# Half-precision activations by a second Gelu on ScalarE, gated sum and latent-key spread on GpSimd

## The chip, the cores and the metric

One core of one Trainium2 chip runs the kernel. The metric is the device time of one execution in microseconds (us). Engines are named as in the profile: PE is TensorE's matmul, PEld its weight load, DVE is VectorE, ACT is ScalarE, POOL is GpSimd, SP is SyncE, which issues the DMAs here.

## The reference

The input x is 16 sequences of 512 tokens of 256 numbers (fp32). A layer of attention with 16 heads of 16 numbers is followed by a feed-forward layer of 1024; each adds its input and ends in a layer norm without gain.

```python
# attention
qkv = x @ qkv_w + qkv_b; q, k, v = split(qkv)
local = window_attention(heads(q), heads(k), heads(v))      # the 128 keys before each query
pooled = x.reshape(B, 64, 8, D).mean(axis=2)                 # 64 latent chunks of 8 tokens
rk, rv = split(pooled @ rkv_w + rkv_b)                       # 4 latent heads of 16
lattn = softmax(mask(rq @ rk.T / 4)); remote = (lattn @ rv) @ rout_w + rout_b
gate = sigmoid(local @ gl_w + remote_h @ gr_w)               # one number per token and head
mixed = gate * local + (1.0 - gate) * remote_h
x = layernorm(x + mixed @ out_w + out_b)
# feed-forward; ternary(w) is sign(w) * (|w| > 0.5 * mean|w|)
h = gelu(rmsnorm(x) @ ternary(w_up).T)                       # exact gelu
x = layernorm(x + rmsnorm(h) @ ternary(w_down).T)
```

## The kernel before

Everything is written by hand for each engine: five instruction streams (`block.sync`, `gpsimd`, `scalar`, `vector`, `tensor`) that wait for each other by semaphores. An engine runs its own stream strictly in the order written. `over_sequences` unrolls the 16 sequences.

A sequence s has a first half and a second half. In the first half (16 units u, `FIRST_HALF`) PE makes the scores of s (L1385) and, for s+1, the scores from which row maxima are taken (L1348, DVE `maxima` L1000); ACT takes the exponential (L760), POOL masks it (L598, L602), PE weighs the values (L1405), and ACT and PE bring the result to token order (L748, L1415). The second half is the list `SECOND_HALF`: steps "F" finish sequence s (gate, mixing, output product, norm, feed-forward), steps "P" prepare sequence s+2 (transpose x, query and key products, latent attention, values). All engines walk the same list, each doing its part of a step. The list begins

```python
("P", X_T), ("F", GATE), ("P", QK), ("F", MIX), ("P", QK + 1), ("P", QK + 2), ("P", QK + 3),
("F", MIX_T), ("P", LAT_IN), ("F", OUT), ("P", VALUES), ("P", VALUES + 1), ("P", LAT_SCORES),
```

and goes on with NORM, XN_T, then eight steps UP with the rest of the latent steps between them, and END. Sequences 14 and 15 have no s+2, so their second half holds only the "F" steps. A prologue (`PROLOGUE`) does the "P" steps of sequences 0 and 1 and makes the ternary weights (`w_step`); POOL's part in it has a reduce over the partitions (`partition_all_reduce`, L636) right behind the QK + 3 step of sequence 0.

The steps that the change touches:

- GATE and MIX. DVE computes the gate from o_tok and rem (L1046 to L1054), then four multiplies `mixed = o_tok * gate`, one per block of 128 tokens (L1058; the profile calls the tensor x, as mixed is x1's memory). POOL multiplies rem by one minus the gate, block by block (L613). In step MIX, behind the DVE part of step QK, DVE adds the two (L1066). PE transposes mixed in step MIX_T (L1439), ACT copies the result to mixT (L774), and PE makes the output product in step OUT (L1230, work<-wout,mixT).
- QK + t, for the four tiles t of queries and keys of s+2. The fp32 product is split into three bf16 terms: ACT makes the first (L703), DVE the remainder (L937, into one of two slots of `qk_rest`, so tile t waits for POOL's step of tile t - 2), ACT rounds that to the second (L710, in the step after), POOL subtracts to make the third (L590).
- LAT_IN. DVE adds the bias to the latent keys (rk_sb, L952) and spreads them over the heads by multiplying with a diagonal mask (lat_bd, L955). PE uses lat_bd in LAT_SCORES (L1287).
- UP + t, for the eight tiles of the feed-forward layer. PE makes the product into one of two PSUM slots of `work` (L1477). ACT makes `hbuf = Gelu(work)` in fp32 (L796), then `Square(hbuf)` back into the PSUM slot (L803; for t = 0 into h_sum). DVE casts hbuf to fp16, h_hi (L1114), and adds the square into h_sum (L1120; the profile calls h_sum oT, whose memory it is), which frees the slot. POOL makes the rest `h_lo = hbuf - h_hi` (L626). PE multiplies both with the down weights two steps later (`TRAIL`, L1424).
- END. PE waits for the last h_sum and sums over the partitions (L1491), DVE scales (L1124), POOL takes the root (L631), and DVE forms the residual (L1134). The next first half waits for that.

The kernel's constant `NF_VEC` counts the marks on the semaphore f_vec per sequence.

Of the kernel before, what the change touches and what calls it, by code (L numbers as in the profile page):

```python
# [56 lines left out]
T_AFTER = (-(-NB * H // 2 // MH) - 1, NM - 1)  # L57
NR = 3
TRAIL = 2
NP_VEC, NF_VEC = 6, 14  # L60

# [138 lines left out]
def build(nc, x, qkv_w, qkv_b, rq_w, rq_b, rkv_w, rkv_b, rout_w, rout_b, out_w, out_b, gl_w, gr_w,  # L202
          w_up, w_down, out):
    with ExitStack() as ctx:
# [3 lines left out]
        def sem(name):  # L208
            return ctx.enter_context(nc.semaphore(name))
# [122 lines left out]
        gate_e = sem("gate_e")  # L332
        gate_g = sem("gate_g")
        rem_part = sem("rem_part")
        mixed_ready = sem("mixed_ready")
        var_ready = sem("var_ready")
        rstd_ready = sem("rstd_ready")
# [175 lines left out]
        def _(pool):  # L513
# [69 lines left out]
            def p_step(s, k):  # L583
                if QK <= k < QK + 4:

                    t = k - QK
                    pool.wait_ge(part1, count(s, 4, t))
                    if t == 0 and not s.first:
                        pool.wait_ge(parts_out, count(s, 2, -1) * 48)
                    pool.tensor_tensor(parts[:, 2, t, :], qk_rest[:, t % 2, :], parts[:, 1, t, :],  # L590
                                       ALU.subtract).then_inc(part2, 1)

            def mask(s, u):
                pt = Pt[:, u % NPT, :, :]
# [12 lines left out]
            def f_step(s, k):  # L607
                if k == GATE:

                    pool.wait_ge(gate_g, count(s, 1, 0))  # L610
                    for b in range(NB):
                        rv = rem[:, s.par, b, 0:D].rearrange("p (h d) -> p h d", h=H)
                        pool.tensor_tensor(rv, rv, gate[:, 2, b, :].unsqueeze(2).to_broadcast([P, H, HD]),  # L613
                                           ALU.mult).then_inc(rem_part, 1)
                if k == OUT:

                    pool.wait_ge(var_ready, count(s, 1, 0))
                    pool.tensor_tensor(rs[:, 0:2, :], rs[:, 3:5, :], power[:, :, :], ALU.pow
                                       ).then_inc(rstd_ready, 1)
                if UP <= k < END:  # L620

                    t = k - UP
                    pool.wait_ge(h_hi_ready, count(s, FT, t))
                    if t >= NR:
                        pool.wait_ge(down_done, count(s, FT, t - NR))
                    pool.tensor_tensor(h_lo[:, t % NR, :], hbuf[:, t % 2, :], h_hi[:, t % NR, :],  # L626
                                       ALU.subtract).then_inc(h_lo_ready, 1)
                if k == END:

                    pool.wait_ge(ssq_mean, count(s, 1, 0))  # L630
                    pool.tensor_tensor(rs[:, 2, :], rs[:, 3, :], power[:, 1, :], ALU.pow).then_inc(hroot, 1)  # L631

            def w_step(j):
                if j == 0:
                    pool.wait_ge(alpha_part, 1)
                    pool.partition_all_reduce(alpha[:, 4:6], alpha[:, 2:4], P, RADD).then_inc(alpha_all, 1)  # L636
                    pool.wait_ge(alpha_all, 1)
                if j == 1:


                    pool.wait_ge(ones_set, 2)
                    exclude_k(1)
                    pool.wait_ge(tern, 2)
                    link(pool.memset(Vp[:, :, :, H * VW:], 0.0))
                    link(pool.memset(in_pairs(Qs[1])[ROWS:P], ONE_PAIR))
                    exclude_q(1)
                    pool.sem_inc(q_consts, 1)
# [36 lines left out]
        def _(act):  # L684
# [80 lines left out]
            def f_step(s, k):  # L765
                if k == GATE:
                    act.wait_ge(gate_z, count(s, 1, 0))
                    nc.scalar.activation(gate[:, 1, :, :], gate[:, 0, :, :], ACT.Exp, scale=-1.0
                                         ).then_inc(gate_e, 1)
                if k == MIX_T:  # L770
                    for t in range(KT):
                        slot, n = work_use(s, "F", t)
                        act.wait_ge(w_full[slot], n + 1)
                        nc.scalar.activation(mixT[:, t, :], work[:, slot, :], ACT.Copy  # L774
                                             ).then_inc(w_taken[slot], 1)
                if k == NORM:

                    for b in range(NB):
                        act.wait_ge(x1_ready, count(s, NB, b))
                        nc.scalar.activation(xn[:, b, :], x1[:, b, :], ACT.Copy, scale=rs[:, 2, b:b + 1]  # L780
                                             ).then_inc(xn_ready, 1)
                if k == XN_T:
                    for t in range(KT):

                        slot, n = work_use(s, "F", 4 + t)
                        act.wait_ge(w_full[slot], n + 1)
                        nc.scalar.activation(xnT[:, 0, t, :], work[:, slot, :], ACT.Copy).then_inc(xn_hi, 1)
                if UP <= k < END:
                    t = k - UP
                    slot, n = work_use(s, "F", 6 + t)  # L790
                    act.wait_ge(w_full[slot], n + 1)
                    if t >= 2:

                        act.wait_ge(h_lo_ready, count(s, FT, t - 2))
                        act.wait_ge(h_sq, count(s, FT, t - 2))
                    gelu = nc.scalar.activation(hbuf[:, t % 2, :], work[:, slot, :], ACT.Gelu)  # L796
                    if t == 0:
                        gelu.then_inc(w_taken[slot], 1)
                        act.wait_ge(w_taken[slot], n + 1)
                    else:  # L800
                        gelu.then_inc(h_act, 1)
                        act.wait_ge(h_act, count(s, FT - 1, t - 1))
                    nc.scalar.activation(h_sum[:, :] if t == 0 else work[:, slot, :], hbuf[:, t % 2, :],  # L803
                                         ACT.Square).then_inc(h_sq, 1)

            def body(s):
                for u in range(FIRST_HALF):
# [30 lines left out]
        def _(dve):  # L838
# [75 lines left out]
            def p_step(s, k):  # L914
# [25 lines left out]
                if k == LAT_IN:  # L940
# [4 lines left out]
                    for i in range(2):  # L945
# [5 lines left out]
                                                       in1=bias[:, :, i, :], op0=ALU.mult, op1=ALU.add)  # L951
                    nc.vector.tensor_scalar(rk_sb[:, :], p_bank(bank)[:, 0:LAT], 1.0 / CHUNK, brk[:, :],  # L952
                                            ALU.mult, ALU.add).then_inc(p_taken[bank], 1)
                    dve.wait_ge(p_taken[bank], n + 1)
                    nc.vector.tensor_tensor(lat_bd[:, :, :],  # L955
                                            rk_sb[:, :].unsqueeze(1).to_broadcast([P, LH, LAT]),
                                            diag_mask[:, :, :], ALU.mult).then_inc(bd_ready, 1)
                if LAT_SCORES <= k < LAT_SCORES + 2:

                    b2 = k - LAT_SCORES  # L960
# [59 lines left out]
            def f_step(s, k):  # L1020
# [17 lines left out]
                if k == GATE:  # L1038
# [16 lines left out]
                    sync()  # L1055

                    for b in range(NB):
                        ins = nc.vector.tensor_tensor(mixed[:, b, :].rearrange("p (h d) -> p h d", h=H),  # L1058
                                                      o_tok[:, b, :, 0:HD],
                                                      a[:, b, :].unsqueeze(2).to_broadcast([P, H, HD]), ALU.mult)  # L1060
                    mark(ins)
                if k == MIX:
                    sync()
                    for b in range(NB):
                        dve.wait_ge(rem_part, count(s, NB, b))
                        nc.vector.tensor_tensor(mixed[:, b, :], mixed[:, b, :], rem[:, s.par, b, 0:D], ALU.add  # L1066
                                                ).then_inc(mixed_ready, 1)
                if k == OUT:

                    dve.wait_ge(xres_done, count(s, NB, NB - 1))  # L1070
# [27 lines left out]
                if k == XN_T:  # L1098
                    for t in range(KT):
# [1 line left out]
                        dve.wait_ge(xn_hi, count(s, KT, t))  # L1101
                        nc.vector.tensor_tensor(xnT[:, 1, t, :], work[:, slot, :], xnT[:, 0, t, :], ALU.subtract  # L1102
                                                ).then_inc(w_taken[slot], 1)
                if UP <= k < END:

                    t = k - UP
                    slot, n = work_use(s, "F", 6 + t)
                    if t == 0:
                        dve.wait_ge(w_taken[slot], n + 1)
                    else:  # L1110
                        dve.wait_ge(h_act, count(s, FT - 1, t - 1))
                    if t >= NR:
                        dve.wait_ge(down_done, count(s, FT, t - NR))
                    nc.vector.tensor_copy(h_hi[:, t % NR, :], hbuf[:, t % 2, :]).then_inc(h_hi_ready, 1)  # L1114
                    if t > 0:
                        if t > 1:
                            prior_slot, m = work_use(s, "F", 6 + t - 1)
                            dve.wait_ge(w_taken[prior_slot], m + 1)
                        dve.wait_ge(h_sq, count(s, FT, t))
                        nc.vector.tensor_tensor(h_sum[:, :], h_sum[:, :], work[:, slot, :], ALU.add  # L1120
                                                ).then_inc(w_taken[slot], 1)
                if k == END:
                    slot, n = take(14)
                    nc.vector.tensor_scalar(rs[:, 3, :], work[:, slot, 0:NB], 1.0 / F, None, ALU.mult  # L1124
# [439 lines left out]
```

## Time and profile before

| | |
|---|---|
| median of 3 runs | 1309.5 us (1309.12 to 1319.59) |
| the profiled execution: its own time | 1306.51 us |
| its span | 1304.8 us |
| mean granted TensorE clock | 0.922 of full |
| instructions | 37906 |
| DMA | 108.08 MB |

The profiled execution is one run of the program with the hardware profiler on. Its span is the time from the first to the last instruction; its own time has 1.7 us around it. All rows quoted are of this execution, in us from the span's start unless marked ns. A busy time counts instructions in work, not waits. "idle before <-" names what the engine waited for.

### The profile page before, as it was taken

How to read it: one execution, taken by the hardware profiler on the slowest of the kernel's cores; microseconds unless marked ns; L12 is line 12 of the kernel's file. 1: busy time of each engine (PE TensorE's matmuls, PEld its weight loads, DVE VectorE, ACT ScalarE, POOL GpSimd, SP SyncE). 2: the span in 40 equal slices, each digit the busy share in tenths (PEclk: the TensorE clock that was granted, in tenths of full speed). 3: DMA queues.
4: the chain of work that ended last, by engine and by line, in shares of the span. 5: the costliest groups of instructions: out<-in, count | busy, mean ns of one | idle time of the engine just before them, and what ended most of it. 6: DMA issues, size and time to landing. Idle time of an engine off the chain costs nothing.

```text
span 1304.8 us, 37906 instructions
## 1 busy us (share of the span) xinstructions
PE 1071.0 (82%) x15776; PEld 685.5 (53%) x15776; DVE 963.8 (74%) x2048; ACT 666.2 (51%) x1026; POOL 686.1 (53%) x870
## 2 busy tenths in 40 slices
PE   2566889798988989897998989899888989795855
PEld 1344555464655556464655556465555646464533
DVE  5856768778787887878787877878787887866445
ACT  1213555564646556464646556364655556462624
POOL 6542637373654736364554637265473737364553
PEclk9778989899998999899999989899998989997887
DMA  5845180735537181644628082543719173541000
GB/s 153 139 79 110 43 139 30 125 64 91 92 75 123 37 134 48 115 82 76 107 66 132 30 136 54 106 76 76 122 44 137 46 120 69 98 68 35 2 18 17
DMA packets 57019, 108.08 MB, mean 83 GB/s; under 512 B 14192, under 2 KB 40944, under 8 KB 53744
## 3 DMA queue, kind: packets, MB, share of 16 engines
q1 hardware_dynamic: 56848, 105.66, 44.1%
q8 instruction: 125, 2.05, 0.7%
q14 instruction: 46, 0.38, 0.1%
HBM read 71.55 MB, written 34.08 MB: 81 GB/s over the span
## 4 chain that ended last, share of the span: by engine, by line
PE 52%; DVE 28%; ACT 9%; issue 4%; POOL 4%; SPq 1%; DMA 1%; DVEq 0%; POOLq 0%; ACTq 0%
PE work L1477 9%; PE oacc L1405 7%; PE oacc L1424 6%; PE work L1230 5%; PE work L1348 5%; PE scores L1385 3%; DVE x L1058 3%; PE work L1415 3%; ACT Pt L760 3%; DVE x L1066 3%; DVE nmax L1000 2%; PE scores L1230 2%; DVE ytok L1134 2%; DVE Pt L966 2%; DVE lat_st L963 2%
## 5 line engine op out<-in xcount | busy, mean ns | idle before, releaser
L760 ACT ACTIVATE Pt<-scores 128x1024 f32<-128x1024 f32 (+1 forms) x256 | 228.3, 914 | 115.4 <-PE oacc L1405 83.2
L626 POOL TENSOR_TENSOR h_lo<-hbuf,h_hi 128x512 f16<-128x512 f32 x128 | 148.3, 1159 | 249.6 <-DVE h_hi L1114 249.6
L1000 DVE TENSOR_REDUCE nmax<-work 128x3 f32<-128x480 f32 x352 | 216.5, 636 | 27.8 <-PE work L1353 23.9
L598 POOL TENSOR_SCALAR_AFFINE_SELECT Pt<-Pt 128x512 f32<-128x512 f32 x256 | 163.2, 638 | 109.6 <-ACT Pt L760 108.1
L1477 PE MATMUL work<-xnT,wup_t 128*128 128x512 f16 x512 | 156.6, 444 | 32.5 <-DVE xnT L1102 32.1
L1348 PE MATMUL work<-Ks,Qs 98*32 98x160 bf16 x4096 | 141.5, 237 | 33.0 <-DVE nmax L1000 28.7
L1405 PE MATMUL oacc<-Pt,Vp 128*32 128x256 f32 (+1 forms) x2048 | 149.6, 359 | 3.5 <-POOL Pt L602 3.0
L1255 PE MATMUL scores<-xT,wqk 128*128 128x512 f32 x256 | 116.5, 609 | 19.3 <-ACT xT L695 19.3
L1385 PE MATMUL scores<-Qs,Ks 100*32 100x160 bf16 (+4 forms) x4096 | 113.7, 228 | 13.5 <-ACT Pt L760 10.1
L602 POOL TENSOR_SCALAR_AFFINE_SELECT Pt<-Pt 128x512 f32<-128x512 f32 x192 | 122.0, 635 | 0.0
L1424 PE MATMUL oacc<-wdn_t,h_hi 128*128 128x256 f16 x512 | 120.2, 276 | 0.2
L1424 PE MATMUL oacc<-wdn_t,h_lo 128*128 128x256 f16 x512 | 120.1, 276 | 0.0
L796 ACT ACTIVATE hbuf<-work 128x512 f32<-128x512 f32 x128 | 76.4, 597 | 84.6 <-PE work L1477 84.6
L1348 PEld LDWEIGHTS work<-Ks,Qs 98*32 98x32 bf16 x4096 | 87.8, 97 | 59.8 <-DVE nmax L1000 43.7
L1114 DVE CAST h_hi<-hbuf 128x512 f16<-128x512 f32 x128 | 65.8, 516 | 68.7 <-ACT hbuf L796 68.7
L590 POOL TENSOR_TENSOR parts<-Pt,parts 128x512 bf16<-128x512 f32 x64 | 74.9, 1181 | 77.4 <-ACT parts L710 70.1
L1477 PEld LDWEIGHTS work<-xnT,wup_t 128*128 128x128 f16 x512 | 51.2, 109 | 103.4 <-issue 74.6
L1385 PEld LDWEIGHTS scores<-Qs,Ks 100*32 100x32 bf16 x4096 | 77.2, 97 | 53.3 <-ACT Pt L760 33.3
L1353 PE MATMUL work<-mask_band,identb 128*32 128x192 bf16 (+1 forms) x1408 | 97.6, 249 | 0.0
L1120 DVE TENSOR_TENSOR oT<-oT,work 128x512 f32<-128x512 f32 x112 | 76.8, 685 | 24.4 <-ACT work L803 24.4
L717 ACT ACTIVATE Pt<-Pt 128x512 f32<-128x512 f32 x32 | 20.1, 629 | 137.8 <-DVE Pt L966 137.8
L1255 PEld LDWEIGHTS scores<-xT,wqk 128*128 128x128 f32 x256 | 48.5, 195 | 76.8 <-issue 71.4
(169 smaller groups left out, 2088.8 us busy)
## 6 DMA issues: line engine op xcount, KB each, us to landing
parts_scratch<-parts SPq DMA_DIRECT2D x96, 256.0 KB, 6.8
Qs<-parts_scratch SPq DMA_DIRECT2D x96, 256.0 KB, 9.2
Ks<-parts_scratch SPq DMA_DIRECT2D x96, 256.0 KB, 8.9
xtok<-L_attn_x SPq DMA_DIRECT2D x16, 512.0 KB, 13.7
xres<-L_attn_x SPq DMA_DIRECT2D x16, 512.0 KB, 14.8
y<-ytok SPq DMA_DIRECT2D x16, 512.0 KB, 3.2
Qs<-L_ffn_w_up SPq DMA_DIRECT2D x1, 1024.0 KB, 5.6
Qs<-L_ffn_w_down SPq DMA_DIRECT2D x1, 1024.0 KB, 7.6
```

Of the source, the lines that this page charges most:

```text
L598: ins = pool.affine_select(out=pt[:, :, 0:P], in_=pt[:, :, 0:P], compare_op=ALU.is_gt, fill=0.0, base=0, pattern=[[0, 4], [1, P]], channel ...
L602: ins = pool.affine_select(out=pt[:, :, P:2 * P], in_=pt[:, :, P:2 * P], compare_op=ALU.is_ge, fill=0.0, base=0, pattern=[[0, 4], [-1, P]] ...
L626: pool.tensor_tensor(h_lo[:, t % NR, :], hbuf[:, t % 2, :], h_hi[:, t % NR, :], ALU.subtract).then_inc(h_lo_ready, 1)
L760: nc.scalar.activation(Pt[:, u % NPT, :, 0:w], scores[:, slot, :, :].rearrange("p k (h q) -> p (k h) q", h=2)[:, :, 0:w], ACT.Exp, scale=S ...
L1000: nc.vector.tensor_reduce(nmax[:, :, :].rearrange("p b h -> p (b h)")[:, first:first + n], work[:, slot, 0:n * BAND].rearrange("p (h c) -> ...
L1255: mm = nc.tensor.matmul(p_bank(bank), wqk[:, t, c * P:(c + 1) * P], xT[:, t, :], start=(t == 0), stop=(t == KT - 1))
L1348: nc.tensor.matmul(work[g * GT:(g + 1) * GT, slot, i * BAND:(i + 1) * BAND], q[0:KA, h, at:at + GT], kk[0:KA, h * S + at:h * S + at + BAND ...
L1353: mm = nc.tensor.matmul(o[:, :, 0:NG + 1:NG, :], identb[:, g * GT:(g + 1) * GT], mask_band[:, :, :].unsqueeze(1).to_broadcast([P, n, 2, GT ...
L1385: mm = nc.tensor.matmul(scores[g * GT:(g + 1) * GT, slot, c // 2, (c % 2) * 2 * P + lo:(c % 2) * 2 * P + hi], kk[0:KB, key + lo:key + lo + ...
L1405: mm = nc.tensor.matmul(oacc[c * PVW:(c + 1) * PVW, hg % 2, j * P:j * P + w], Vp[:, s.par, j, h * VW:h * VW + PVW], Pt[:, v % NPT, c, 0:w] ...
L1424: mm = nc.tensor.matmul(oacc[:, b // 2, (b % 2) * D:(b % 2 + 1) * D], (h_hi, h_lo)[j][:, f % NR, b * P:(b + 1) * P], wdn_t[:, f, :], start ...
L1477: mm = nc.tensor.matmul(work[:, slot, :], wup_t[:, t, f * P:(f + 1) * P], xnT[:, part, t, :], start=(part == 0 and t == 0), stop=(part == ...
```

## The change

DVE loses three kinds of instructions. (1) The cast to h_hi goes; ACT makes h_hi by a second Gelu from the same PSUM slot, between the first Gelu and the Square, and the Square now waits for it, as it overwrites the slot. (2) The MIX additions go; POOL makes them in step GATE, each behind its own multiply of the same block and behind DVE's multiply. (3) The spread of the latent keys goes; POOL makes it in LAT_IN. The order of the steps, the buffers and PE's work stay.

```diff
@@ POOL, p_step
+                if k == LAT_IN:
+                    bank, n = p_use(s, R_RKV)
+                    pool.wait_ge(p_taken[bank], n + 1)
+                    pool.tensor_tensor(lat_bd[:, :, :], rk_sb[:, :].unsqueeze(1).to_broadcast([P, LH, LAT]),
+                                       diag_mask[:, :, :], ALU.mult).then_inc(bd_ready, 1)
@@ POOL, f_step, GATE, in the loop over b
                         pool.tensor_tensor(rv, rv, gate[:, 2, b, :].unsqueeze(2).to_broadcast([P, H, HD]),
                                            ALU.mult).then_inc(rem_part, 1)
+                        pool.wait_ge(rem_part, count(s, NB, b))
+                        pool.wait_ge(mixed_part, count(s, NB, b))
+                        pool.tensor_tensor(mixed[:, b, :], mixed[:, b, :], rem[:, s.par, b, 0:D], ALU.add
+                                           ).then_inc(mixed_ready, 1)
@@ POOL, f_step, UP
+                    pool.wait_ge(h_act, count(s, FT, t))
                     pool.wait_ge(h_hi_ready, count(s, FT, t))
@@ POOL, w_step, j == 1
+                    pool.wait_ge(bd_ready, 1)
                     pool.wait_ge(ones_set, 2)
@@ ACT, f_step, UP
                         act.wait_ge(h_lo_ready, count(s, FT, t - 2))
-                        act.wait_ge(h_sq, count(s, FT, t - 2))
-                    gelu = nc.scalar.activation(hbuf[:, t % 2, :], work[:, slot, :], ACT.Gelu)
+                        if t == 2:
+                            first_slot, m = work_use(s, "F", 6)
+                            act.wait_ge(w_taken[first_slot], m + 1)
+                        else:
+                            act.wait_ge(h_sq, count(s, FT - 1, t - 3))
+                    nc.scalar.activation(hbuf[:, t % 2, :], work[:, slot, :], ACT.Gelu).then_inc(h_act, 1)
+                    if t >= NR:
+                        act.wait_ge(down_done, count(s, FT, t - NR))
+                    nc.scalar.activation(h_hi[:, t % NR, :], work[:, slot, :], ACT.Gelu).then_inc(h_hi_ready, 1)
+                    act.wait_ge(h_act, count(s, FT, t))
                     if t == 0:
-                        gelu.then_inc(w_taken[slot], 1)
-                        act.wait_ge(w_taken[slot], n + 1)
+                        nc.scalar.activation(h_sum[:, :], hbuf[:, t % 2, :], ACT.Square
+                                             ).then_inc(w_taken[slot], 1)
                     else:
-                        gelu.then_inc(h_act, 1)
-                        act.wait_ge(h_act, count(s, FT - 1, t - 1))
-                    nc.scalar.activation(h_sum[:, :] if t == 0 else work[:, slot, :], hbuf[:, t % 2, :],
-                                         ACT.Square).then_inc(h_sq, 1)
+                        act.wait_ge(h_hi_ready, count(s, FT, t))
+                        nc.scalar.activation(work[:, slot, :], hbuf[:, t % 2, :], ACT.Square).then_inc(h_sq, 1)
@@ DVE, p_step, LAT_IN
-                    dve.wait_ge(p_taken[bank], n + 1)
-                    nc.vector.tensor_tensor(lat_bd[:, :, :],
-                                            rk_sb[:, :].unsqueeze(1).to_broadcast([P, LH, LAT]),
-                                            diag_mask[:, :, :], ALU.mult).then_inc(bd_ready, 1)
@@ DVE, f_step, GATE: each of the four multiplies now increments mixed_part
-                        ins = nc.vector.tensor_tensor(mixed[:, b, :].rearrange("p (h d) -> p h d", h=H),
...
-                    mark(ins)
-                if k == MIX:
-                    sync()
-                    for b in range(NB):
-                        dve.wait_ge(rem_part, count(s, NB, b))
-                        nc.vector.tensor_tensor(mixed[:, b, :], mixed[:, b, :], rem[:, s.par, b, 0:D], ALU.add
-                                                ).then_inc(mixed_ready, 1)
+                        nc.vector.tensor_tensor(mixed[:, b, :].rearrange("p (h d) -> p h d", h=H),
...
+                                                ).then_inc(mixed_part, 1)
@@ DVE, f_step, UP: the cast goes, the sum stays
-                if UP <= k < END:
+                if UP < k < END:
...
-                    nc.vector.tensor_copy(h_hi[:, t % NR, :], hbuf[:, t % 2, :]).then_inc(h_hi_ready, 1)
-                    if t > 0:
...
+                    prior_slot, m = work_use(s, "F", 6 + t - 1)
+                    dve.wait_ge(w_taken[prior_slot], m + 1)
+                    dve.wait_ge(h_sq, count(s, FT - 1, t - 1))
+                    nc.vector.tensor_tensor(h_sum[:, :], h_sum[:, :], work[:, slot, :], ALU.add
+                                            ).then_inc(w_taken[slot], 1)
```

## Rows read from the trace of the kernel before

**Rows 1.** The page: engine, busy us, share of the span, instructions.
```profile
PE 1071.0 (82%) x15776; PEld 685.5 (53%) x15776; DVE 963.8 (74%) x2048; ACT 666.2 (51%) x1026; POOL 686.1 (53%) x870
```

**Rows 2.** Timeline of DVE at three of the sixteen residuals: start, us, engine, line, operation, tiles, shapes, count.
```profile
196.33 1.66 DVE L1134 SCALAR_TENSOR_TENSOR ytok<-oacc,rs,x 128x256 f32<-128x256 f32 x4
...
714.25 1.66 DVE L1134 SCALAR_TENSOR_TENSOR ytok<-oacc,rs,x 128x256 f32<-128x256 f32 x4
...
1086.60 1.66 DVE L1134 SCALAR_TENSOR_TENSOR ytok<-oacc,rs,x 128x256 f32<-128x256 f32 x4
```

**Rows 3.** Chain that ended last, front of one period: start, us, what.
```profile
599.21 2.19 DVE x L1066 x4
...
605.09 3.69 PE work L1230 x16
```

**Rows 4.** Timeline of ACT, the same front.
```profile
603.40 0.62 ACT L710 ACTIVATE parts<-Pt 128x512 bf16<-128x512 f32 x1
603.91 1.07 ACT L774 ACTIVATE mixT<-work 128x512 f32<-128x512 f32 x2
```

**Rows 5.** Chain that ended last, tail of the same period.
```profile
636.23 0.61 ACT hbuf L796
636.85 0.61 ACT work L803
637.56 0.70 DVE oT L1120
...
641.15 1.66 DVE ytok L1134 x4
```

**Rows 6.** Timeline of POOL, the same front: in brackets the idle time before.
```profile
594.83 3.04 POOL L613 TENSOR_TENSOR rem<-rem,gate 128x256 f32<-128x256 f32 x4 [3.06 <-DVE gate L1054]
600.04 1.27 POOL L590 TENSOR_TENSOR parts<-Pt,parts 128x512 bf16<-128x512 f32 x1 [2.18 <-ACT parts L710]
603.00 2.27 POOL L590 TENSOR_TENSOR parts<-Pt,parts 128x512 bf16<-128x512 f32 x2 [1.69 <-ACT parts L710]
```

**Rows 7.** Groups of instructions by line: count, busy us, mean ns, idle before.
```profile
L653 POOL TENSOR_TENSOR xres<-xres,bout 128x256 f32<-128x256 f32 x64 | 44.5, 727 | 0.0
```

**Rows 8.** Two lines of DVE by themselves: count, ns min/median/max, first and last start.
```profile
L1058 DVE TENSOR_TENSOR x<-o_tok,gate x64: 424/837/847, 148.8 to 1257.2; 128x256 f32<-128x256 f32 x64
L955 DVE TENSOR_TENSOR lat_bd<-rk_sb,diag_mask x16: 424/1154/1157, 43.0 to 1125.8; 128x256 f32<-128x256 f32 x16
```

**Rows 9.** Prologue: timeline and chain, and a configuration record of POOL's queue (ns, start).
```profile
43.95 1.85 PE L1287 MATMUL scores<-lat_bd,rqT 64*128 64x256 f32 x8 [0.28 <-DVE Vp L974]
...
46.98 0.41 POOL L636 PARTITION_ALL_REDUCE alpha<-alpha  x1 [7.87 <-issue]
...
53.07 1.88 DVE L881 TENSOR_SCALAR alpha<-alpha 128x2 f32<-128x2 f32 x1
...
L590 POOLq MODIFY_POOL_CONFIG  x2: 11/11/11, 74.4 to 74.4; - x2
...
76.92 0.53 ACT parts L710
...
81.44 2.26 POOL L590 TENSOR_TENSOR parts<-Pt,parts 128x512 bf16<-128x512 f32 x2 [7.29 <-issue]
```

**Rows 10.** Timeline of ACT in the UP steps of the same period.
```profile
623.07 0.60 ACT L803 ACTIVATE work<-hbuf 128x512 f32<-128x512 f32 x1
623.61 0.58 ACT L723 ACTIVATE Pt<-scores 128x512 f32<-128x512 f32 x1
...
636.23 0.60 ACT L796 ACTIVATE hbuf<-work 128x512 f32<-128x512 f32 x1 [0.51 <-PE work L1477]
```

**Rows 11.** Timeline of POOL and of ACT, front of sequence 14.
```profile
1189.65 3.03 POOL L613 TENSOR_TENSOR rem<-rem,gate 128x256 f32<-128x256 f32 x4 [2.98 <-DVE gate L1054]
...
1194.87 1.09 ACT L774 ACTIVATE mixT<-work 128x512 f32<-128x512 f32 x2 [6.48 <-PE work L1439]
```

More of the change, by code:

```diff
@@ L59 @@
 TRAIL = 2
-NP_VEC, NF_VEC = 6, 14
+NP_VEC, NF_VEC = 6, 13
 X_T, QK, LAT_IN, LAT_SCORES, VALUES, LAT_NORM, LAT_T, LAT_O, REMOTE = 0, 1, 5, 6, 8, 12, 13, 15, 16
@@ L334, in build @@
         rem_part = sem("rem_part")
+        mixed_part = sem("mixed_part")
         mixed_ready = sem("mixed_ready")
@@ L1057, in f_step @@
                     for b in range(NB):
-                        ins = nc.vector.tensor_tensor(mixed[:, b, :].rearrange("p (h d) -> p h d", h=H),
-                                                      o_tok[:, b, :, 0:HD],
-                                                      a[:, b, :].unsqueeze(2).to_broadcast([P, H, HD]), ALU.mult)
-                    mark(ins)
-                if k == MIX:
-                    sync()
-                    for b in range(NB):
-                        dve.wait_ge(rem_part, count(s, NB, b))
-                        nc.vector.tensor_tensor(mixed[:, b, :], mixed[:, b, :], rem[:, s.par, b, 0:D], ALU.add
-                                                ).then_inc(mixed_ready, 1)
+                        nc.vector.tensor_tensor(mixed[:, b, :].rearrange("p (h d) -> p h d", h=H),
+                                                o_tok[:, b, :, 0:HD],
+                                                a[:, b, :].unsqueeze(2).to_broadcast([P, H, HD]), ALU.mult
+                                                ).then_inc(mixed_part, 1)
                 if k == OUT:
@@ L1103, in f_step @@
                                                 ).then_inc(w_taken[slot], 1)
-                if UP <= k < END:
+                if UP < k < END:
                     t = k - UP
                     slot, n = work_use(s, "F", 6 + t)
[L1108 to L1113, printed above, removed]
-                    nc.vector.tensor_copy(h_hi[:, t % NR, :], hbuf[:, t % 2, :]).then_inc(h_hi_ready, 1)
-                    if t > 0:
[L1116 to L1121, printed above, removed]
+                    prior_slot, m = work_use(s, "F", 6 + t - 1)
[3 more added lines that the diff above has]
+                                            ).then_inc(w_taken[slot], 1)
                 if k == END:
```

## The prediction

> **What bounds the kernel now.** I read the page's busy table first. DVE is busy for 963.8 us, 74% of the span, and ACT for 666.2 us, 51% [rows 1], so the change looks like work taken from the fuller engine. But shares are averages over stages, so I went on to the chain of waits. The work is one long pattern repeated per sequence. Between the final residual (L1134) of the first and of the thirteenth sequence stand 1086.60 - 196.33 = 890.3 us, 74.2 us for each of twelve [rows 2]. I took one period (590.4 to 664.3) and followed its two places that the change touches.
>
> The front of the period, from the gate to the output product, is a hand-over. The reader is to see DVE's four MIX adds on the chain (2.19 us from 599.21) and the product L1230 on PE at 605.09 [rows 3]; between them ACT copies the third part at 603.40 and mixT at 603.91 [rows 4]. From there the chain stays on PE through VALUES and the latent scores, so whatever moves L1230 moves the rest. The tail is a chain too: the last Gelu at 636.23, its Square at 636.85, DVE's sum at 637.56, then the column sums, the root, and L1134 at 641.15 [rows 5]. PE runs its queue in order behind the column sums, and the next period starts from there. A period is therefore longer by whatever either place loses.
>
> **MIX adds to POOL.** POOL's four multiplies start at 594.83 and take 3.04 us, 0.76 each beside DVE [rows 6]. The added instruction is a plain 128x256 fp32 add; the nearest row is the bias add L653, 727 ns [rows 7]. Each add waits for its own multiply, so the pair doesn't overlap: about 0.80 + 0.76 = 1.56 us, four pairs 6.2 us, POOL free at 594.83 + 6.2 = 601.0. Behind them in POOL's queue stands L590, which makes the last of the three bf16 terms of a part. It began at 600.04 when ACT had finished the first one's rounded copy [rows 6]; now it begins at 601.0 and ends 1.16 later (half of the pair's 2.27 with the overlap), at 602.2. DVE, freed of 2.19 us, does the second remainder at once (599.2 to 599.9), but the third waits for that L590 (its buffer has two slots): 602.3 to 603.05. ACT's copy of it starts at 603.1 where it started 603.4, behind ACT's other copy [rows 4]. mixT and L1230 come 0.25 us earlier. So 2.19 us leave DVE and 0.25 us leave the path; the next thing late is POOL's L590. Bounds: eight instructions at the 0.70 of back-to-back ones (0.727 less the overlap) end at 600.4, and the gain is 0.8; at 0.85 each, DVE's 0.837 under contention [rows 8], they end at 601.6, and the loss is 0.3. I take -0.25 us, by the nearest rows.
>
> DVE's own multiplies pay for POOL already: L1058 takes 424 ns at best and 837 ns at the median, L955 424 and 1154 [rows 8]. POOL's 0.76 spacing already holds that meeting. DVE's later instructions there read PSUM and one SBUF tensor, and I charge no more contention.
>
> The Trainium skill has two rules against the move. GPSIMD Engine Reference, section 4.1, says that a two-input elementwise instruction is about twice as slow there as on VectorE; here the ratio is 727 to 424, 1.7. Its section 8 says that GpSimd shares its SBUF interfaces with VectorE instructions of two SBUF inputs; the two levels of L1058 agree.
>
> **Latent keys to POOL.** In a steady period L955 leaves DVE (1.15 us, of which some 0.7 was waiting for POOL), but DVE then waits for L1230's second half anyway: nothing gained. On POOL it runs behind the last L590, about 0.79 us, done two microseconds before PE's latent scores want it: nothing lost. The cover is PE's output product and VALUES; without it the cost would be those 0.8 us.
>
> In the prologue it is different. POOL's first step there behind the fourth part is the cross-partition reduce L636, and the new product stands right behind it, before the exclude memsets. The trace shows POOL changing its code: a configuration record at 74.4 and the next TENSOR_TENSOR only at 81.44, 7.0 us later, though ACT's copy had been done at 76.92 + 0.53 = 77.45; and 7.87 us of idle before L636 itself [rows 9]. Before, memsets came behind the reduce, and the record stands behind the last of them. Now it stands at 47.4: lat_bd runs from 54.4 to 55.2, and PE's latent scores, at 43.95 [rows 9], start 11.3 us later. DVE's queue follows; it gives back the 1.8 us that L881 lost beside a memset [rows 9], so the ternary work and the second sequence's products come 9.5 us later: ACT's copy is ready at 86.9. The code is by then in place, so L590 starts at 86.9 and not at 81.44: +5.5 us. DVE's 0.42 in the second sequence is within that error. Bounds: +2.5 if lat_bd needs no change back (it then ends at 48.2, and 4.3 less 1.8 remain), +6.5 if it takes the 7.9 of the other idle.
>
> The same page of the Trainium skill, section 2.1, gives about 6 us for loading freshly called code; the trace's 7.0 is longer, and by 6 us the term would be 4.5.
>
> **Second Gelu on ACT.** Eight casts leave DVE, eight Gelus join ACT. POOL's h_lo can start about as before. Inside UP the steps of PE (four up and eight down matmuls, and a latent step in many) set the pace; ACT's three instructions fit: a Gelu takes 0.60 us, and independent instructions overlap by 0.06 (0.60 long, 0.54 apart) [rows 10], so the second adds 0.54. The Square waits for it, since it overwrites the PSUM slot that both read, so its latency shows: 0.56 in all. At the last step nothing hides that. ACT was idle just 0.51 us before the last Gelu [rows 10]; the step before is now 0.56 longer and spills 0.05. The tail gets +0.56 + 0.05 = +0.6 us per sequence. DVE's cast was not on that chain, so nothing is given back. Bounds: 0.5 (full overlap) to 0.9 (latent copies push ACT too).
>
> **The last two sequences** have no following sequence's steps to hide under. DVE's adds fed the transposes at once and mixT started at 1194.87; POOL's multiplies started at 1189.65 [rows 11]. With eight on POOL the last ends 6.2 later, 1195.85, the two transposes and the hand-over take 0.55, mixT starts at 1196.4: +1.5 each, between +0.9 and +2.
>
> **Sum.** 14 x (-0.25 + 0.6) = +4.9; the last two 2 x (1.5 + 0.6) = +4.2; prologue +5.5. Together +14.6 us. On the profiled execution, 1304.8 span and 1306.5 in all, that is 1321.1; the median shown is 1309.5, 3.0 above it, and the forecast is **1324 us**, 1.1% slower. A measurement of this kernel can tell about 1% (13 us) from no change.
>
> **Rivals.**
> - *DVE's queue was the bound, and its 2.19 us go whole.* The place is the front, 599.21 to 601.4 [rows 3]. Then 14 x -2.19 = -30.7, with the other terms 14 x 0.6 + 4.2 + 5.5 = +18.1: -12.6, 1297 us. For it: DVE is the fuller engine and the adds are on the chain. Against it: L590 can't begin before 600.04, when its part comes, and ends 1.16 later, so the front can give at most 1.2. It decides from POOL ending its eight before 600. Chance 0.08. With just the 1.2 it would be 1311, inside my range.
> - *PE's clock.* Two stretches in which PE waits get longer (the tail by 0.6, the front's transposes spread out), and the pattern is uneven already: one period took 714.25 - 641.15 = 73.1 [rows 2, 5] against the mean of 74.2. If half-clock stretches grow by as much as the good period lacks them, 14 x 1.1 = +15: 1339; half of it 1331. Chance 0.17.
> - *ACT becomes the bound inside UP.* It has 24 instructions and three latent copies there. If the latent product waits 0.3 for ACT and the end slips by 0.3 more: 14 x 0.6 = +8.4, 1332. Chance 0.15. Against it: 0.51 us of idle before even the last Gelu [rows 10], nearly the 0.54 that a step adds.
> - *POOL slower than its rows* (a wait on its own result costs more): +0.55 in each front, +1 in the last two: +9.7, 1334. Chance 0.1.
>
> My own case has 0.5, 1314 to 1330. The threshold for slower by over 1% is 1322.6, so its half and most of three rivals lie above it: 0.55 slower, 0.39 same, 0.06 faster. Range 1309 to 1336.
>
> **What would show it.** Right: L590's first start at about 601 and POOL as its releaser; L1230 0.2 to 0.3 earlier after the gate; from the last Gelu to L1134 5.5 us instead of 4.9; a configuration record on POOL at 47 and lat_bd near 54, L590 of the second sequence near 87; ACT busy 128 x 0.60 = 77 us more, and DVE less. Wrong: the first L590 still at 600.0, or PE's column sums not later after the last up matmul, or lat_bd right behind the reduce.

## The result and the profile after

The changed kernel takes 1331.6 us (median of four runs, 1328.2 to 1336.2) against 1309.3 us for the kernel before: a ratio of 1.0173, 95% interval 1.0108 to 1.0239, 22.3 us longer. The forecast was 1324. The profiled executions lie 24.7 us of span apart (1329.5 against 1304.8), with a granted clock of 0.912 against 0.922.

The page of the changed kernel, busy time and granted clock in 40 slices:
```profile
PE 1074.8 (81%) x15776; PEld 692.8 (52%) x15776; DVE 851.9 (64%) x1840; ACT 720.3 (54%) x1154; POOL 742.5 (56%) x950
PEclk9687989889888999899998999899998999897977
```
Against [rows 1] DVE has lost 112 us and ACT and POOL have gained 54 and 56, and the kernel is slower. The work went where it was meant to go; only the chain can say what that was worth.

**The front.** Timeline of POOL, the front of the same sequence as [rows 6]:
```profile
612.33 0.76 POOL L619 TENSOR_TENSOR rem<-rem,gate 128x256 f32<-128x256 f32 x1 [3.05 <-DVE gate L1069]
613.16 0.79 POOL L623 TENSOR_TENSOR x<-x,rem 128x256 f32<-128x256 f32 x1
...
616.92 0.62 POOL L619 TENSOR_TENSOR rem<-rem,gate 128x256 f32<-128x256 f32 x1
617.62 0.72 POOL L623 TENSOR_TENSOR x<-x,rem 128x256 f32<-128x256 f32 x1
618.30 2.28 POOL L591 TENSOR_TENSOR parts<-Pt,parts 128x512 bf16<-128x512 f32 x2
```
The eight instructions take 5.97 us (612.33 to 618.30); the prediction had 6.2. As it said, the next thing late is POOL's own L591, and the chain of waits goes on from there:
```profile
618.34 1.13 POOL parts L591
619.60 0.76 DVE Pt L956
620.38 0.63 ACT parts L722
621.01 0.98 ACT mixT L786 x2
622.08 3.69 PE work L1230 x16
...
694.90 5.63 PE work L1230 x16
```
From POOL's first multiply to the product it was 605.09 - 594.83 = 10.26 us, and is 622.08 - 612.33 = 9.75. The last line is the same product one sequence later, 5.63 us instead of 3.69. The stretches show the clock of both products, and of the time just before the later one (columns: length, busy time of PE, PEld, DVE, ACT and POOL with instructions, granted clock, DMA share, GB/s):
```profile
622.00:626.00 4.00, 3.92 (x18) 3.48 (x19) 2.07 (x6) 0.50 (x1) 2.08 (x3) 1.00 0.70 124
691.00:694.00 3.00, 2.78 (x26) 1.91 (x26) 1.23 (x2) 1.88 (x4) 2.48 (x4) 0.67 0.23 87
694.90:700.50 5.60, 5.60 (x17) 4.60 (x18) 1.79 (x5) 0.42 (x1) 1.99 (x3) 0.65 0.88 144
```
A granted clock of 1.00 is 2.4 GHz; 0.65 is a stretch mostly at 1.2 GHz. What PE did before it, on its timeline:
```profile
688.43 0.60 PE L1439 MATMUL work<-ident,x 128*128 128x128 f32 x4
689.84 0.44 PE L1439 MATMUL work<-ident,x 128*128 128x128 f32 x2 [0.81 <-POOL x L623]
691.22 0.44 PE L1439 MATMUL work<-ident,x 128*128 128x128 f32 x2 [0.94 <-POOL x L623]
```
In the kernel before, in the period of [rows 3], they were:
```profile
599.77 1.02 PE L1439 MATMUL work<-ident,x 128*128 128x128 f32 x6 [1.51 <-DVE x L1066]
601.65 0.44 PE L1439 MATMUL work<-ident,x 128*128 128x128 f32 x2 [0.86 <-DVE x L1066]
```
There the transposes came six together after one wait of 1.51 us and two after another of 0.86; now they come as POOL finishes each block. These pieces alone don't decide: the same three, with the same two waits, stand ahead of the product at 622.08, which ran at full clock.

**The tail.** Chain of waits, answering to [rows 5]:
```profile
652.14 0.60 ACT hbuf L812
652.74 0.50 ACT h_hi L815
653.32 0.61 ACT work L823
654.03 0.70 DVE oT L1120
654.77 1.07 PE work L1491 x8
...
657.62 1.66 DVE ytok L1134 x4
```
From the last Gelu to L1134 it was 4.92 us and is 5.48: +0.56.

**The prologue.** POOL's timeline, with its configuration records between the first two instructions (ns, start):
```profile
46.50 0.40 POOL L647 PARTITION_ALL_REDUCE alpha<-alpha  x1 [7.94 <-issue]
...
L596 POOLq MODIFY_POOL_CONFIG  x2: 83/83/83, 46.9 to 46.9; - x2
...
53.52 0.71 POOL L596 TENSOR_TENSOR lat_bd<-rk_sb,diag_mask 128x256 f32<-128x256 f32 x1 [6.62 <-issue]
...
84.94 1.16 POOL L591 TENSOR_TENSOR parts<-Pt,parts 128x512 bf16<-128x512 f32 x1 [2.01 <-ACT parts L722]
```
A configuration record stands right behind the reduce, and 6.6 us pass before lat_bd. The Trainium skill (GPSIMD Engine Reference, 2.1 Instruction dispatch) gives about 6 us for loading code at the first call to a freshly loaded kernel of GpSimd; from the record to the next instruction it is a little longer, 6.6 us here and 7.0 in [rows 9].

**By stage.** To put all periods side by side I cut each sequence, on the timelines of DVE, PE and ACT, at five events: the first reciprocal of the gate (called the gate below), the first matmul of the output product, DVE's first write of xnT, the last Gelu, the residual L1134. The fifth stage runs to the next gate. Means over sequences 1 to 12, in us, and the time of the first gate:

| kernel | gate to product | to xnT | to last Gelu | to L1134 | to next gate | first gate at |
|---|---|---|---|---|---|---|
| before | 12.93 | 13.21 | 17.76 | 4.93 | 25.40 | 146.3 |
| changed | 12.42 | 13.77 | 17.76 | 5.47 | 25.84 | 153.0 |

The period before was 74.2 and is 75.3. At full clock the second and fifth stages take 12.95 and 24.9 at best in both kernels, so their rises are clock, not work: the second is 1.5 us or more above its best once in the twelve sequences before and five times after, the fifth three times and six times. In sequences 14 and 15 the first stage rose from 9.08 to 10.40 and the third from 14.4 to 15.3.

### The profile page after: what moved, and what is told of

It reads as the page before. It is cut to its first block, busy times and chain, and to the rows that moved or that the text cites. A ratio compares the mean times of both kernels' runs of the same rounds, so it can differ in the third digit from the quotient of the medians.

```text
span 1329.5 us, 38051 instructions
## 1 busy us (share of the span) xinstructions
PE 1074.8 (81%) x15776; PEld 692.8 (52%) x15776; DVE 851.9 (64%) x1840; ACT 720.3 (54%) x1154; POOL 742.5 (56%) x950
## 4 chain that ended last, share of the span: by engine, by line
PE 51%; DVE 21%; POOL 11%; ACT 10%; issue 5%; SPq 1%; DMA 1%; DVEq 0%; POOLq 0%; ACTq 0%
PE work L1477 9%; PE oacc L1405 7%; PE work L1230 6%; PE work L1348 5%; PE oacc L1424 5%; PE scores L1385 3%; POOL rem L619 3%; POOL x L623 3%; PE work L1415 3%; ACT Pt L772 2%; DVE nmax L1015 2%; PE scores L1230 2%; DVE ytok L1134 2%; DVE Pt L981 2%; PE work L1353 2%
## 5 line engine op out<-in xcount | busy, mean ns | idle before, releaser
L637 POOL TENSOR_TENSOR h_lo<-hbuf,h_hi 128x512 f16<-128x512 f32 x128 | 154.3, 1207 | 243.9 <-ACT h_hi L815 233.9
L1477 PE MATMUL work<-xnT,wup_t 128*128 128x512 f16 x512 | 150.6, 429 | 33.8 <-DVE xnT L1111 32.1
L1405 PE MATMUL oacc<-Pt,Vp 128*32 128x256 f32 (+1 forms) x2048 | 152.5, 367 | 3.4 <-POOL Pt L608 3.1
L1230 PE MATMUL work<-wout,mixT 128*128 128x256 f32 x256 | 75.5, 460 | 20.4 <-ACT mixT L786 20.4
L591 POOL TENSOR_TENSOR parts<-Pt,parts 128x512 bf16<-128x512 f32 x64 | 73.4, 1158 | 22.8 <-ACT parts L722 22.8
```

The lines of the kernel that those rows point to most:

```text
L1230: mm = nc.tensor.matmul(out, lhs(t), rhs(t), start=(t == 0), stop=(t == n - 1))
L1405: mm = nc.tensor.matmul(oacc[c * PVW:(c + 1) * PVW, hg % 2, j * P:j * P + w], Vp[:, s.par, j, h * VW:h * VW + PVW], Pt[:, v % NPT, c, 0:w] ...
L1477: mm = nc.tensor.matmul(work[:, slot, :], wup_t[:, t, f * P:(f + 1) * P], xnT[:, part, t, :], start=(part == 0 and t == 0), stop=(part == ...
```

## The experiments

Theory A (the prediction's): what is slower is the edits' own, namely the tail, the prologue, the last two sequences. Theory B: the edits are small, and most of the loss is TensorE at half clock. "Idle work" below is unused matmuls into a bank of PSUM that the next real product overwrites. All times by stage are of one profiled execution of each kernel.

**1. The second Gelu alone** (adds and spread back on DVE).
```diff
@@ POOL, f_step, GATE
-                        pool.tensor_tensor(mixed[:, b, :], mixed[:, b, :], rem[:, s.par, b, 0:D], ALU.add
-                                           ).then_inc(mixed_ready, 1)
@@ DVE, f_step
+                if k == MIX:
+                    for b in range(NB):
+                        dve.wait_ge(mixed_part, count(s, NB, b))
+                        dve.wait_ge(rem_part, count(s, NB, b))
+                        nc.vector.tensor_tensor(mixed[:, b, :], mixed[:, b, :], rem[:, s.par, b, 0:D], ALU.add
+                                                ).then_inc(mixed_ready, 1)
```


> The second Gelu alone; additions and latent spread stay on DVE. Stage theory: from the last Gelu to the residual 5.48 us in place of 4.92, 16 x 0.55 = +8.8 us, 1318; no other stage moves at full clock. If the added waits of PE in the tail are what brings half-clock stretches behind it, as much again (0.44 x 14 = +6, 1324). Rival, the half-clock stretches fall by chance of the period's length: +9 with up to 10 either way, and then not behind the tail in particular. Rival, ACT is the bound inside UP: the stretch from xnT to the last Gelu longer than 17.3 at full clock.


Measured: 1320.8 us, 1.0131 [1.0085, 1.0176]. The tail stage is 5.48, as in the changed kernel. The stage to the next gate is 25.39, as before, so its rise in the changed kernel's trace isn't brought by the Gelu alone. The whole is some 17 us by the ratio, about twice the tail's 16 x 0.55 = 8.8, with a mean granted clock of 0.919 over its runs against 0.923.

**2. The additions alone** (spread and cast on DVE).
```diff
@@ ACT, f_step, UP
-                    nc.scalar.activation(h_hi[:, t % NR, :], work[:, slot, :], ACT.Gelu).then_inc(h_hi_ready, 1)
@@ DVE, f_step
+                if UP <= k < END:
...
+                    nc.vector.tensor_copy(h_hi[:, t % NR, :], hbuf[:, t % 2, :]).then_inc(h_hi_ready, 1)
```


> The MIX additions alone on GpSimd. Stage theory: gate to output product 12.42 us in place of 12.93 in 14 periods (-7.2), 1.33 more in the last two (+2.7): -4.5 us, 1305 (ratio 0.9966), the tail unchanged at 4.92. If the spread transposes cost clock at the output product (0.56 x 14 = +8): 1313. Rival, GpSimd saved the front nothing and only the latent spread's removal did: 12.93 stays.


Measured: 1313.0, 1.0053 [1.0026, 1.0080]. Its gate-to-product stage is 12.42, half a microsecond shorter than before, and yet the kernel is slower, as expected for the case that the spread transposes cost clock. The second stage takes 13.76, and the mean granted clock over ten runs is 0.905, against 0.923 before, 0.919 with the Gelu alone and 0.921 with the spread alone.

**3. The spread alone**: the diffs of 1 and 2 for the additions and the cast, with lat_bd left on POOL.


> The latent spread alone on GpSimd. Code-change theory: the first gate 6 to 7 us later (152.5 to 153 in place of 146.3), every period unchanged: +6.5 us, 1316. Rival, the prologue's loss is a queue effect of the single product: +0.7 us. Rival, the spread also sets the front: gate to output product shorter than 12.93.


Measured: 1315.0, 1.0084 [1.0047, 1.0121]; the first gate is at 153.6 instead of 146.3.

**4. The change, with the spread of the first two sequences on DVE.**
```diff
-                if k == LAT_IN:
+                if k == LAT_IN and s.i >= 2:
```


> The changed kernel with the latent spread of the first two sequences on DVE again, all else as changed. Code-change theory: first gate back at 146.3, -6.5 us against the changed kernel, 1325 (ratio to before 1.012). Rival: GpSimd changes its code at that place anyway and the first gate stays near 153.


Measured: the first gate at 148.7 (146.3 was expected; the kernels with that spread on DVE have 146.3 to 149.0), but 1332.1 in the median, 1.0218 [1.0166, 1.0269]. Its five executions are the plainest sign of the clock: one took 1317.0 us with a mean granted clock of 0.920, the other four 1331.7 to 1335.7 with 0.909 to 0.910. One program, one input, 15 us. The profile is of the first of them. What decides between the two levels stayed open.

The clock's price at the product can be read in one group, all 256 of its matmuls: before, gelu_only, the changed kernel, adds_only:
```profile
L1230 PE MATMUL work<-wout,mixT 128*128 128x256 f32 x256 | 66.9, 420 | 13.3 <-ACT mixT L774 13.0
```
```profile
L1230 PE MATMUL work<-wout,mixT 128*128 128x256 f32 x256 | 67.5, 423 | 16.4 <-ACT mixT L776 16.1 <-issue 0.2
```
```profile
L1230 PE MATMUL work<-wout,mixT 128*128 128x256 f32 x256 | 75.5, 460 | 20.4 <-ACT mixT L786 20.4
```
```profile
L1230 PE MATMUL work<-wout,mixT 128*128 128x256 f32 x256 | 72.9, 448 | 20.8 <-ACT mixT L780 20.8
```
One takes 379 ns in the median of every kernel. With the adds on DVE the mean is 417 to 423 (three kernels); with them on POOL 430 to 483 (the changed kernel, adds_only, spread_steady, and mended below). So the lower clock at the product goes with the adds. That it comes from the transposes' broken stream needs a kernel in which only PE's idle time changes.

**5 and 6. Idle work in the changed kernel, and in the kernel before.**
```diff
+            def idle_work(n):
+                for _ in range(n):
+                    nc.tensor.matmul(oacc[:, 0, :], wup_t[:, 0, 0:P], wup_t[:, 0, 0:512], start=True, stop=True)
@@ PE, step OUT, ahead of the waits of the output product
+                    idle_work(6)
@@ PE, first UP step, ahead of its wait for xnT
+                    idle_work(8)
```


> The changed kernel with matmuls that nobody reads in two of PE's waits: 6 of 128x512 fp16 ahead of the output product, 8 ahead of the first up product (their results are overwritten). Clock theory: the half-clock stretches at the output product and behind xnT come from PE's waits there; with PE busy they go, mean wout to xnT 12.95 in place of 13.77, and the stretch behind xnT loses its half-clock part; the whole 10 to 15 us below the changed kernel, 1317 to 1322. Rival, the clock falls by chance or by total activity: the same share of half clock (0.91), and the time as before or longer by the matmuls that overrun the waits.

> The kernel before with the same idle matmuls. Clock theory: 4 to 10 us faster than before (mean period 74.2 to 73.3 or less), since its 0.5 us of half clock per period at these places goes as well. Rival: no change or slower, as the 6 matmuls take 1.3 us of a 1.5 us wait and delay the output product when they run at half clock.


Measured: the changed kernel 1307.4, 1.0029 [1.0001, 1.0057]; the kernel before 1303.5, 0.9995 [0.9971, 1.0018]. With 14 matmuls more per sequence the changed kernel goes from 1.0173 to 1.0029 of the kernel before, 1.4% or 19 us (by the ratios, since the chips differ); its mean clock over ten runs is 0.954, from 0.913 over four. Its page:
```profile
PEclk9777999999999999999999999999999999997978
```
So theory B holds for this kernel: only PE's idle time was touched, and most of the loss is gone. The product's group, changed kernel, then before, both with idle work:
```profile
L1230 PE MATMUL work<-wout,mixT 128*128 128x256 f32 x256 | 60.3, 390 | 2.5 <-ACT mixT L786 2.5
```
```profile
L1230 PE MATMUL work<-wout,mixT 128*128 128x256 f32 x256 | 58.3, 381 | 0.5
```
The kernel before gained nothing, against what I expected: the same six matmuls end after mixT is ready (its gate-to-product stage is 13.90, up from 12.93, in nine of twelve periods 14.2), because the front itself fell to half clock there. The half-clock stretch had moved. In UP the two differ also at full clock: 17.45 us before, 17.13 changed. The waits of the kernel before with idle work (us, times, longest) name it:
```profile
PE oacc L1428 <- POOL h_lo L626: 3.7, 16, 0.7
PEld oacc L1428 <- POOL h_lo L626: 11.5, 16, 1.1
```
PE's down product waits for the low part once in each sequence; in the changed kernel this wait comes twice in the whole span, 0.5 us in all. The second Gelu gives h_hi, and by it h_lo, earlier than DVE's cast did. It is the Gelu and not the adds: at full clock UP takes 17.11 in gelu_only and 17.45 in adds_only.

**7 and 8. Mended**: the spread stays on DVE, the adds of the last two sequences go back to DVE, and the cast of the last of the eight tiles too; 8 adds the idle work of 5.
```diff
+                        if s.i < B - 2:
                             pool.wait_ge(rem_part, count(s, NB, b))
...
+                    if t < FT - 1:
                         nc.scalar.activation(h_hi[:, t % NR, :], work[:, slot, :], ACT.Gelu).then_inc(h_hi_ready, 1)
```


> The changed kernel without its three losses: latent spread on DVE throughout, additions of sequences 14 and 15 on DVE, and the cast of the last of the eight tiles on DVE, so that its Square follows the first Gelu at once. Stage theory: tail 4.92 again, front 12.42, last two fronts 9.08, first gate 146 to 149: 14 x -0.51 = -7 us against before, ratio 0.994. Rival: the seven remaining second Gelus still cost, stretch xnT to last Gelu longer than 17.3 at full clock, ratio 1.000 or more.

> Both together: the mended kernel with the idle matmuls. If the clock theory holds: ratio 0.98 to 0.987. If the clock doesn't follow PE's waits: as the mended kernel, 0.994, or above.


Measured: mended 1312.7, 1.0070 [1.0041, 1.0098]; with idle work 1290.6, 0.9899 [0.9848, 0.9950], a little above the 0.98 to 0.987 expected. The tail is 4.93 again, the first gate at 147.8, the first stage 12.41 (9.1 in the last two sequences): every loss that theory A named is taken back, and the kernel is still slower than before until PE's idle time is filled. One loss that the prediction hadn't named is left: the third stage of the last two sequences still takes 15.4, against 14.4 before. Its product is the slowest of all:
```profile
L1241 PE MATMUL work<-wout,mixT 128*128 128x256 f32 x256 | 80.4, 483 | 15.4 <-ACT mixT L781 15.4
```

**9 to 12. How many matmuls, and where.** Mended with 3 at the product and 8 at UP, with 0 and 8, and with them spread over the waits; the kernel before with 3 and 8. The third:
```diff
@@ PE, step MIX_T, ahead of the wait for mixed_ready of block b
+                        if b >= 2:
+                            idle_work(2)
@@ PE, step OUT
+                    idle_work(4)
@@ PE, first UP step
+                    idle_work(8)
```


> As mended_idle_work with 3 idle matmuls ahead of the output product in place of 6. In the run with 6 the front took 13.49 us in half of the periods and 12.41 in the others: at half clock 6 x 0.43 = 2.6 us overrun the wait of 1.8. With 3 (1.3 us at half clock) they fit. If the front still shields the output product: front 12.41 everywhere and wout to xnT 12.9, 0.5 us per period better, 1283. Rival: 3 are too few, the half clock comes back to the output product (wout to xnT 14.9 in some periods), 1290 to 1295.

> The mended kernel with the 8 idle matmuls ahead of the first up product only. Place theory: the wait in the front rules the output product, the wait behind xnT rules the up products, each for itself: wout to xnT 14.9 in about half the periods as in the mended kernel, xnT to last Gelu 17.10: 1300. Rival, the wait behind xnT rules both: 1283 to 1287.

> The mended kernel with the front's idle matmuls spread over its three waits (2 ahead of the third and the fourth block's transposes, 4 ahead of the output product) and 8 ahead of the first up product. If PE's three waits together are what lowers the clock in the front: no half clock there, front 12.41, wout to xnT 12.9, all of it at 0.96 or more: 1281 to 1284. Rival: no better than 6 in one place, 1290.

> The kernel before with 3 idle matmuls ahead of the output product and 8 ahead of the first up product. With 6 its front went from 12.93 to 14.2 in nine of twelve periods and so gave back what the clock had won. If they fit now: front 12.93 and a mean period of 73.1, 1292 (ratio 0.991). Rival: half clock at the output product again, 1300.

| kernel | us | ratio to before, 95% | clock, mean of runs | gate to product | to xnT | product, mean ns |
|---|---|---|---|---|---|---|
| mended_3_8 | 1292.4 | 0.9856 [0.9812, 0.9899] | 0.952 | 12.48 | 13.11 | 393 |
| mended_0_8 | 1294.9 | 0.9884 [0.9845, 0.9923] | 0.950 | 12.41 | 13.47 | 443 |
| mended_spread_8 | 1286.9 | 0.9823 [0.9779, 0.9867] | 0.966 | 12.41 | 12.95 | 383 |
| before_3_8 | 1299.5 | 0.9941 [0.9909, 0.9973] | 0.952 | 13.26 | 12.99 | 394 |

Three of the four are slower than expected (1283, 1281 to 1284 and 1292 for the first, third and fourth); only mended_0_8 is faster than its 1300. In mended_3_8 and before_3_8 half clock shows also in the fifth stage, which holds no idle work: 25.7 and 25.6, against 25.3 in mended_spread_8.

The eight at UP do most of it. What the front's waits do at the product shows between mended_0_8 and mended_spread_8, which differ in the idle work of the front alone: a matmul of the product takes 443 ns in the mean and then 383, and the second stage 13.47 and then 12.95. With the waits filled, no matmul of the product takes more than 454 ns (766 before), and the front keeps its 12.41. Two stretches of this kernel, then of the changed one:
```profile
600.00:750.00 150.00, 135.38 (x2026) 86.84 (x2025) 107.63 (x244) 88.33 (x142) 89.38 (x111) 1.00 0.51 90
750.00:900.00 150.00, 134.98 (x2020) 85.61 (x2018) 107.42 (x243) 92.00 (x150) 87.75 (x110) 1.00 0.51 90
```
```profile
600.00:750.00 150.00, 130.38 (x1972) 84.33 (x1968) 101.94 (x227) 89.56 (x145) 87.65 (x112) 0.94 0.47 87
750.00:900.00 150.00, 130.22 (x1968) 84.57 (x1961) 101.78 (x227) 89.26 (x145) 87.63 (x113) 0.94 0.47 87
```
At 1286.9 us mended_spread_8 is faster than both kernels: it is 1.8% below the one before by the ratio, and 1.4% by the medians (1305.4 for that kernel in the same rounds). Its eight matmuls at the front differ from mended_idle_work's six in number as well as in place, and the two weren't separated. Idle work in the tail, where TensorE also waits, was not tried.

## Why the prediction came out as it did

The time lay in the range, 7.6 us above the forecast. Partly this is luck: two errors that cancel. By its own steps:

- **MIX adds, "I take -0.25 us".** Right in mechanism (the next thing late is POOL's L591), under-sized: -0.51 per period. The pair was priced at 1.56 us throughout; it costs that only while DVE's multiplies run beside it. The last two multiplies take 0.62 us, so POOL is free after 5.97, and the hand-over behind it was a little shorter too.
- **"Nothing is given back" for the Gelu.** Wrong at full clock: the UP steps are 0.3 us shorter (17.45 to 17.13, both with idle work), as PE no longer waits for h_lo. A period with half clock in UP doesn't give it back: those with 6 to 7 us of it take 18.0 to 18.2 or 19.2 to 19.4 before and after alike, and the mean of the stage is 17.76 in both. So +0.54 - 0.3 is the Gelu's price per period at full clock only; alone the second Gelu measured 1.0131.
- **Tail, "+0.6".** Right: +0.55. The spill of 0.05 is absent. One sign came out otherwise: ACT's busy time grew by 54 us, not by 77.
- **Latent keys, steady.** Right as far as the best periods tell: spread_only's first, second and fourth stages are those of before, and the third has its best periods at 17.40, where before has 17.34. Its mean is 18.47 against 17.76, with more half clock in it.
- **Prologue, "+5.5".** Right in size: the first gate is at 153.2 in the mean of the three kernels with this spread on POOL, and at 147.9 in the eleven without, +5.3. The steps fit less well: lat_bd was expected at 54.4 and came at 53.5; L591 of the second sequence at 86.9, and came at 84.9, which is 3.5 and not 5.5 behind the 81.44 of before. The last of its four parts ends 4.2 later (90.6 against 86.5), and what adds the rest up to the gate wasn't followed.
- **Last two sequences, "+1.5 each" and the tail.** +1.33 and +0.55, but about +1.0 each was missed in the third stage (gelu_only has it too, 15.4 and 15.7 against 14.4 and 14.3). There no latent or score step stands between PE's products, and ACT becomes the bound, which the prediction held as a rival only for UP with latent copies. ACT's timeline in the last sequence:
```profile
1303.28 0.60 ACT L812 ACTIVATE hbuf<-work 128x512 f32<-128x512 f32 x1
1303.77 0.59 ACT L815 ACTIVATE h_hi<-work 128x512 f16<-128x512 f32 x1
1304.46 0.60 ACT L823 ACTIVATE work<-hbuf 128x512 f32<-128x512 f32 x1
1304.99 0.58 ACT L812 ACTIVATE hbuf<-work 128x512 f32<-128x512 f32 x1
```
  One tile each 1.71 us (1304.99 - 1303.28), with 0.1 us idle at most between two instructions.
- **The clock, a rival at 0.17 with "+15".** This is the step that failed: the sum has no term for the clock. The edits as measured, at full clock, sum to 14 x (-0.51 + 0.55 - 0.3) = -3.6, prologue +5.3, last two 2 x (1.33 + 0.55 + 1.0) = +5.8: +7.5 us, not 14.6. The medians are 22.3 apart, so some 15 us are left over, the size that the rival had. They are a remainder, not a measurement. The stages give about as much by another way: 14 x (0.56 + 0.44) = 14 us for the second and the fifth. The adds alone tell the same: their edits sum to 14 x -0.51 + 2 x 1.33 = -4.5 us and they measured +7 (0.53%), so 11 us went to the clock. And with PE's waits filled in both, the changed kernel (1.0029) lies 4 us above the kernel before with the same numbers (0.9995), 12 above it with the better ones (0.9941), not 22; the 7.5 of the edits is between. What was shown is that filling PE's idle time gives 19 us back in the changed kernel (1.0173 to 1.0029), 22 in the mended one (1312.7 to 1290.6, on one chip) and, with the better of two numbers, 8 in the kernel before (1.0 to 0.9941). The prediction named the very cause (the tail longer, "the front's transposes spread out") and gave it too little, because it had no row that priced it. Such a row was there, the product by itself in the kernel before (ns min/median/max):
```profile
L1230 PE MATMUL work<-wout,mixT x256: 379/379/766, 159.2 to 1267.3; 128*128 128x256 f32 x128
```

The forecast was thus close through edit terms 7 us too high and a clock term, put at nothing, some 15 us too low.

## What to carry to other kernels

Before work is moved off a busy engine, ask what stands next behind it on the chain: here 112 us taken from DVE were worth half a microsecond a period. Look at whether the move breaks up TensorE's work or lengthens its waits; in this kernel the clock lost that way cost about twice as much as every edit together (an estimate, 15 us against 7.5). Where waits can't be removed, a few unused matmuls in each of them can pay, if each group is shorter than its wait and stands at it: six in one place overran the wait in five to nine of twelve periods, and there the half-clock stretch stood in the front.

## What I had not expected of the hardware

- POOL's two-input 128x256 fp32 multiply takes 0.62 us once DVE's multiplies are over and 0.76 to 0.80 beside them (614 to 802 ns over 64). The add, L623, is between 722 and 792.
- The first ordinary TENSOR_TENSOR behind POOL's cross-partition reduce came 6.6 to 7.0 us after its configuration record, while before the change a memset stood behind the same reduce and began at once (at 47.44, the reduce ending at 47.39).
- One program's executions differed by 15 us with their granted clock (spread_steady, 0.920 and 0.910). The kernel before itself ran from 1298 to 1320 us over all its runs.
